# Gate and hid products by Strassen's scheme over 1024 tokens, with weights streamed per slice

## The chip, the cores and the metric

The kernel runs on one core of one Trainium2 chip. The metric is the device time of one launch in microseconds, as a median over runs. In the text PE is TensorE, ACT is ScalarE, DVE is VectorE, POOL is GpSimd, and SP is the queue that issues most DMAs.

## The reference

For 4 batches of 1024 tokens, 512 features each, the result is x plus one transformer block (all in float32):

```
x = x + attention(rmsnorm(x, t; g1, b1))          # 16 heads of 32
h = rmsnorm(x, t; g2, b2)                         # gain and bias from the condition t
y = (silu(h @ gate_w.T) * (h @ hid_w.T)) @ out_w.T    # hidden size 2048
out = x_in + (x + y)
```

The change touches only the second stage, from the second rmsnorm to the end.

## The kernel before

The kernel is two programs in sequence. `attention_program` computes the attention of all 4 batches and stores it to a DRAM tensor (`attn_out`). `ffn_program` does the rest. Each is a block in which every engine has its own instruction stream, with semaphores between them, written out by hand. Every product is taken with three matmuls: an operand is split into a rounded part (hi, written by ACT as float32r) and the rest (lo, written by DVE as full minus hi), and hi·hi, hi·lo and lo·hi are summed in PSUM.

`ffn_program` works on half batches of 512 tokens. At its start SP loads all weights: `wT` (gate and hid, 128 rows by 16 slices by 2 by 512) and `woT`. They stay in SBUF. Per half batch there are 16 slices `j` of 128 hidden units. In a slice:

- ACT rounds the two weight tiles of the next slice (L1113) and one of out_w (L1132); DVE takes the rests (L1189, L1211).
- PE makes two tiles of 128 by 512, gate and hid, with 4 k-tiles times 3 matmuls each, 24 in all (L1306), into a ring of four PSUM banks.
- ACT takes silu of gate from PSUM (L1137), DVE multiplies by hid from PSUM (L1217), ACT rounds the result (L1139), DVE takes its rest (L1221).
- PE adds the slice's part of the output product with 4 times 3 matmuls, 12 in all (L1287), one slice behind.

Beside this the next half batch is prepared: POOL adds x and attention, 128 by 2048 elements in one instruction, and the residual (L1084, L1086), ACT squares (L1102), DVE scales (L1170), and in slices 8 to 11 PE transposes one k-tile each (L1267, 16 transposes a half batch), which ACT and DVE split (L1107, L1180, L1183). After slice 15 DVE adds the four output banks to the residual (L1237) and SP stores them. For the first half batch this preparation stands ahead of the loop.

The first stage ends with 8 output tiles of 128 tokens (L776, L758), stored by SP; POOL issues the second stage's first loads while it ends (L420), each held back by a count of finished tiles, and waits for them at the end of its stream.

## Time and profile before

| | |
|---|---|
| median of 3 runs | 2622.42 us (2621.76 to 2624.55) |
| profiled execution | 2623.54 us |
| its span, first to last instruction | 2621.7 us |
| mean granted TensorE clock, share of full speed | 0.987 |
| second stage, first matmul of a slice to the last | 1547.6 to 2616.3 us |
| PE, DVE, ACT, POOL busy in that stretch | 1064.1, 544.7, 413.5, 88.2 us |

Durations of matmuls overlap: a matmul of 512 columns is shown as some 390 ns long, while one starts every 227 ns. What a stretch of them takes is to be read from start to start. "Idle before" is how long an engine stood still ahead of such an instruction, and what ended most of it.

### The profile page before, as it was taken

The numbers are of one execution on the slowest core, as the hardware profiler recorded it, in microseconds if no ns is written. First come the engines' busy times: TensorE is split into PE (matmuls) and PEld (weight loads), VectorE is DVE, ScalarE is ACT, GpSimd is POOL, SyncE is SP. The second block draws the span as 40 slices with busy tenths as digits, with TensorE's granted clock in tenths as the row PEclk, the third lists the DMA queues.
The fourth block names the chain that finished last, engine by engine and source line by source line (L and its number), as shares of the span: only waits on it lengthen the run. The fifth ranks groups of instructions, "written<-read, shape, count | busy, mean of one in ns | idle before, by whom it ended". The sixth has DMA issues, their size and how long they took to land. (4 is left out here: it accounts for less than half of the span.)

```text
span 2621.7 us, 38622 instructions
## 1 busy us (share of the span) xinstructions
PE 2474.9 (94%) x11764; PEld 1651.4 (63%) x11764; DVE 1478.8 (56%) x2316; ACT 1261.1 (48%) x2206; POOL 755.0 (29%) x557
## 2 busy tenths in 40 slices
PE   5999989999989999899999869999999999999999
PEld 4644437544446544365444448888888888888887
DVE  4766735667736667446677354554545454545454
ACT  4455662566653556625566524344434333343343
POOL 0255550455541555514555510000101010101010
PEclk8999999999999999999999979999999999999999
DMA  5222103212132112032121260101010101000000
GB/s 197 49 47 55 57 13 102 49 45 58 45 93 53 42 43 64 29 102 46 40 65 45 87 271 1 49 1 50 1 49 1 48 3 38 12 24 27 17 33 17
DMA packets 56685, 135.18 MB, mean 52 GB/s; under 512 B 11664, under 2 KB 11664, under 8 KB 53136
## 3 DMA queue, kind: packets, MB, share of 16 engines
q1 hardware_dynamic: 55920, 130.34, 16.7%
q8 instruction: 113, 1.85, 0.3%
q0 software_dynamic: 544, 2.10, 0.2%
q14 instruction: 108, 0.88, 0.1%
HBM read 59.78 MB, written 19.92 MB: 30 GB/s over the span
## 5 line engine op out<-in xcount | busy, mean ns | idle before, releaser
L409 POOL TENSOR_TENSOR sums<-probs 128x512 f32<-128x512 f32 x512 | 653.1, 1301 | 790.2 <-ACT probs L560 788.5
L633 DVE TENSOR_REDUCE pmax<-bank 128x1 f32<-128x512 f32 x1024 | 655.0, 685 | 279.5 <-PE bank L838 268.3
L560 ACT ACTIVATE probs<-bank 128x512 f32<-128x512 f32 x1024 | 584.1, 597 | 403.8 <-PE bank L921 370.2
L921 PE MATMUL bank<-qs,ks 128*128 128x512 f32 x1024 | 458.9, 453 | 29.2 <-ACT probs L560 28.5
L921 PEld LDWEIGHTS bank<-qs,ks 128*128 128x128 f32 x1024 | 191.3, 188 | 373.0 <-ACT probs L560 225.4
L838 PE MATMUL bank<-ks,qs 96*128 96x512 f32 x1024 | 401.1, 404 | 25.6 <-DVE pmax L633 25.5
L1306 PE MATMUL bank<-h_hi,gu_hi 128*128 128x512 f32 x1024 | 400.1, 391 | 9.3 <-DVE h_lo L1183 4.8
L1306 PE MATMUL bank<-h_hi,gu_lo 128*128 128x512 f32 x1024 | 399.5, 390 | 0.0
L1306 PE MATMUL bank<-h_lo,gu_hi 128*128 128x512 f32 x1024 | 399.4, 390 | 0.0
L1217 DVE TENSOR_TENSOR sg<-bank,sg 128x512 f32<-128x512 f32 x128 | 88.5, 691 | 385.2 <-PE bank L1306 385.2
L861 PE MATMUL bank<-probs,v 128*32 128x512 f32 x2048 | 275.9, 611 | 8.0 <-ACT o L492 5.3
L1139 ACT ACTIVATE a_hi<-sg 128x512 fp32r<-128x512 f32 x128 | 80.9, 632 | 386.9 <-DVE sg L1217 386.9
L838 PEld LDWEIGHTS bank<-ks,qs 96*128 96x128 f32 x1024 | 193.8, 189 | 73.0 <-DVE pmax L633 46.7
L1084 POOL TENSOR_TENSOR x<-x,res 128x2048 f32<-128x2048 f32 x8 | 38.2, 4770 | 668.5 <-DMA x<-attn_out 668.5
L1306 PEld LDWEIGHTS bank<-h_hi,gu_hi 128*128 128x128 f32 x1024 | 192.9, 188 | 51.5 <-issue 11.4
L1306 PEld LDWEIGHTS bank<-h_hi,gu_lo 128*128 128x128 f32 x1024 | 192.9, 188 | 40.2
L1306 PEld LDWEIGHTS bank<-h_lo,gu_hi 128*128 128x128 f32 x1024 | 192.9, 188 | 39.9
L1287 PE MATMUL bank<-wo_hi,a_hi 128*128 128x512 f32 x512 | 202.5, 396 | 0.0
L1287 PE MATMUL bank<-wo_hi,a_lo 128*128 128x512 f32 x512 | 199.6, 390 | 0.0
L1287 PE MATMUL bank<-wo_lo,a_hi 128*128 128x512 f32 x512 | 199.2, 389 | 0.0
L1189 DVE TENSOR_TENSOR gu_lo<-wT,gu_hi 128x512 fp32r<-128x512 f32 x258 | 188.2, 771 | 11.7 <-ACT gu_hi L1113 9.9
L1137 ACT ACTIVATE sg<-bank 128x512 f32<-128x512 f32 x128 | 76.3, 596 | 244.9 <-PE bank L1306 244.9
(108 smaller groups left out, 2767.4 us busy)
## 6 DMA issues: line engine op xcount, KB each, us to landing
ks<-qk_hi SPq DMA_DIRECT2D x136, 128.0 KB, 2.4
qs<-qk_hi SPq DMA_DIRECT2D x264, 64.0 KB, 2.0
x<-in_x SPq DMA_DIRECT2D x10, 1024.0 KB, 5.5
ks<-qk_lo SPq DMA_DIRECT2D x68, 128.0 KB, 2.4
qs<-qk_lo SPq DMA_DIRECT2D x132, 64.0 KB, 2.0
wv<-wv_parts SPq DMA_DIRECT2D x4, 2048.0 KB, 9.1
attn_out<-yout SPq DMA_DIRECT2D x32, 256.0 KB, 2.6
wT<-in_gu_w SPq DMA_DIRECT2D x8, 1024.0 KB, 14.2
```

The lines of the kernel that those rows point to most:

```text
L409: nc.gpsimd.tensor_tensor(sums[:, h, :], probs[:, 0, h, :], probs[:, 1, h, :], ALU.add) \
L560: nc.scalar.activation(probs[:, s % 2, h, :], sbank[i % SB][:], ACT.Exp, scale=SCALE).then_inc(st_done, 1)
L633: nc.vector.reduce_max(pmax[:, t, h, hf:hf + 1], mbank[n % MB][:], AX_X).then_inc(sq_done, 1)
L838: nc.tensor.matmul(mbank[n % MB][:], qs[0:96, u % 3, h, t * P:(t + 1) * P], ks[0:96, u // 2 % 2, h, hf * QB:(hf + 1) * QB], start=True, st ...
L861: last = nc.tensor.matmul(obank[DH * h:DH * h + DH, :], v[:, s, (g * GH + h) * DH:(g * GH + h + 1) * DH], probs[:, s % 2, h, :], start=(s ...
L921: nc.tensor.matmul(sbank[i % SB][:], ks[:, g % 2, h, s * P:(s + 1) * P], qs[:, u % 3, h, :], start=True, stop=True).then_inc(st_ready, 1)
L1137: nc.scalar.activation(sg[:, j % 2, :], psum[n % GU_BANKS][:], ACT.Silu).then_inc(g_act, 1)
L1139: nc.scalar.activation(a[0][:, j % 2, :], sg[:, j % 2, :], ACT.Copy).then_inc(ah, 1)
L1189: nc.vector.tensor_tensor(gu[1][:, slot, w, :, :], wT[:, j, w, :, :], gu[0][:, slot, w, :, :].bitcast(F32), ALU.subtract).then_inc(gul, 1)
L1217: nc.vector.tensor_tensor(sg[:, j % 2, :], psum[n % GU_BANKS][:], sg[:, j % 2, :], ALU.mult).then_inc(prod, 1)
L1287: last = nc.tensor.matmul(ybank[t][:], a[p][:, j % 2, t * P:(t + 1) * P], wo[q][:, j % 2, :], start=(j == 0 and p == 0 and q == 0), stop=( ...
L1306: last = nc.tensor.matmul(psum[n % GU_BANKS][:], gu[p][:, j % 2, w, k, :], hT[q][:, hf, k, :], start=(i == 0), stop=(i == len(steps) - 1))
```

## The change

The second stage now handles a whole batch of 1024 tokens at a time, in two phases.

Phase one, the gate and hid products. In each of the 16 slices the weights are a 2 by 2 matrix of blocks (gate or hid, by first or second half of the 512 features), and the activations are a 2 by 2 matrix (half of the features, by half of the tokens). Instead of 8 block products there are 7, each with 2 k-tiles times 3 matmuls, 42 in a slice for 1024 tokens. The operands are combinations. Those of the activations (`T1` to `T4`) are made once a batch by DVE; those of the weights (`S1` to `S4`) are made for every slice of every batch by POOL (`combos`), rounded by ACT in one instruction of 1024 columns, and their rests are taken by POOL too (`combos_lo`), eight POOL instructions of 128 by 256 a slice. The blocks used as they are (`A11`, `A12`, `A22`) are rounded by ACT and their rests taken by DVE (`weight_lo`). The seven products use four banks of one parity of `j`; three of the banks are used by two or three products in turn. ACT copies the first product out (`p1_copied`), and DVE makes seven sums with one operand in PSUM: `c11`, `u2`, `p5`, `c22`, `u3`, `c12`, `c21`. Then follow two silus on ACT (`gate1`, `gate2`) and two multiplications on DVE with both operands in SBUF (`gated`). Results for all 16 slices are kept in SBUF in full precision (`a`). The next batch's x and attention are added, squared and scaled in slices 4 to 7, 5 to 8 and 11 to 14, two tiles of 128 by 512 each; the adding is now DVE's.

Phase two, the output product, in 32 steps of 12 matmuls: 16 slices for the first 512 tokens, then 16 for the second. For each step ACT rounds a tile of `a` and one of out_w and DVE takes the rests, in rings of three. Beside it the next batch's 8 tiles are transposed, normalised by ACT (`full_tile`), combined by DVE and split. x and attention are loaded again for the residual.

Weights are no longer kept: SP loads 512 KB a slice (`load_raw`, a ring of three) and 256 KB an output step (`load_wo`, a ring of two). The lead prepares all 1024 tokens of batch 0, from four early loads in place of two. The core of the diff (both engines' loops in the middle of it without the removed lines, which are those printed above):

```diff
-                pool.wait_ge(sq_ready, NB * (NU * NMAX + NT) - NT + 3 * n + 1)
+                pool.wait_ge(sq_ready, NB * (NU * NMAX + NT) - NT + 2 * n + 1)
...
+A11, A12, A22, S1, S2, S3, S4 = range(NP)
+B11, B21, B22, T1, T2, T3, T4 = range(NP)
+PRODUCTS = ((A11, B11, 0), (A12, B21, 1), (S2, T2, 0), (S1, T1, 2), (S3, T3, 3), (S4, B22, 1), (A22, T4, 0))
+QUAD = ((0, 0), (2, 0), (2, 1), (0, 1))
+SPLIT_ORDER = (B11, B21, B22, T1, T3, T2, T4)
+T_ORDER = (T1, T3, T2, T4)
+TILES_AT = {q: (0, q) for q in range(4)} | {9 + q: (1, q) for q in range(4)}
+FULL_AT = {n + 2: tile for n, tile in TILES_AT.items()}
...
+                hold(sp, held, w_lo, b * (2 * NJ) + 2)
+                load_raw(2)
+                hold(sp, held, out_mm, b * STEPS + 1)
+                load_raw(3)
+                load_raw(4)
+                hold(sp, held, s_lo, b * (4 * NJ) + 8)
+                hold(sp, held, w_lo, b * (2 * NJ) + 4)
+                for s in y_stored:
+                    hold(sp, held, s, b * 32 + 16)
+                for hf in range(2):
+                    sp.dma_start(x1[:, TPH * hf:TPH * (hf + 1), :], tokens(attn, prepared, hf)).then_inc(x_loaded[hf], 16)
+                    sp.dma_start(xr[:, TPH * hf:TPH * (hf + 1), :], tokens(x, prepared, hf)).then_inc(x_loaded[hf], 16)
+                for j in range(5, NJ):
+                    hold(sp, held, w_lo, b * (2 * NJ) + 2 * (j - 2))
+                    hold(sp, held, s_step, b * (4 * NJ) + 4 * (j - 2))
+                    load_raw(j)
+                for n in range(STEPS):
+                    load_wo(b, n)
+                    if n == 2:
+                        load_raw(0)
+                    if n == 17:
+                        hold(sp, held, h_full, b * 8 + 16)
+                        for t in range(TPH):
+                            load_pair(b, 0, t)
+                    if n == 21:
+                        hold(sp, held, h_lo, b * (2 * NP) + 4 * NP)
+                        load_raw(1)
+                    if n >= STEPS - 6 and n < STEPS - 2:
+                        store(b, 0, n - (STEPS - 6))
+                    if n >= STEPS - 4:
+                        hold(sp, held, y_stored[n - (STEPS - 4)], b * 32 + 32)
+                        load_pair(b, 1, n - (STEPS - 4))
...
+            def combos(b, j, lead=False):
+                w = b * (4 * NJ) + 4 * j
+                src, to = raw_place(j), s_place(j, lead)
+                a11, a12, a21, a22 = src[:, 0, 0:2, :], src[:, 0, 2:4, :], src[:, 1, 0:2, :], src[:, 1, 2:4, :]
+                pool.wait_ge(raw_loaded[raw_sem(j)], raw_count(b, j))
+                nc.gpsimd.tensor_tensor(to[:, 0], a21, a22, ALU.add).then_inc(s_step, 1)
+                nc.gpsimd.tensor_tensor(to[:, 2], a11, a21, ALU.subtract).then_inc(s_step, 1)
+                pool.wait_ge(s_step, w + 1)
+                nc.gpsimd.tensor_tensor(to[:, 1], to[:, 0], a11, ALU.subtract).then_inc(s_step, 1)
+                pool.wait_ge(s_step, w + 3)
+                nc.gpsimd.tensor_tensor(to[:, 3], a12, to[:, 1], ALU.subtract).then_inc(s_step, 1)
...
+            def combos_lo(b, j, lead=False):
+                src, (hi, lo) = s_place(j, lead), wt[j % 2]
+                pool.wait_ge(w_hi, b * (3 * NJ) + 3 * (j + 1))
+                for i in range(4):
+                    nc.gpsimd.tensor_tensor(lo[:, S1 + i], src[:, i], hi[:, S1 + i].bitcast(F32),
+                                            ALU.subtract).then_inc(s_lo, 1)
...
+                for j in range(1, NJ):
+                    combos_lo(b, j)
+                    if j == 1:
+                        pool.wait_ge(out_mm, b * STEPS + 1)
+                    if j < NJ - 1:
+                        pool.wait_ge(s_lo, b * (4 * NJ) + 4 * (j + 1))
+                        combos(b, j + 1)
+                    if j == 11:
+                        inverse_root(b + 1)
+                pool.wait_ge(h_lo, b * (2 * NP) + 4 * NP)
+                combos(b + 1, 0)
+                combos_lo(b + 1, 0)
...
+            weight_hi(0, 0, True)
+            for t in range(8):
                 square(0, t)
+            for i in range(2):
+                for q in range(4):
+                    full_tile(0, i, q)
+                    if q < 3:
+                        h_rounded(0, i, (q,))
+                h_rounded(0, i, T_ORDER)
             with act.Fori(0, NB) as b:
+                for j in range(NJ):
+                    if j < NJ - 1:
+                        weight_hi(b, j + 1, False, (0, 1))
+                    act.wait_ge(prod_done, b * (NP * NJ) + NP * j + 1)
+                    nc.scalar.activation(a[:, j, 0, :], psum[4 * (j % 2)][:], ACT.Copy).then_inc(p1_copied, 1)
+                    if j < NJ - 1:
+                        weight_hi(b, j + 1, False, (2,))
+                    else:
+                        a_rounded(b, 0)
+                        wo_rounded(b, 0)
+                        wo_rounded(b, 1)
+                    act.wait_ge(c11_done, b * NJ + (j + 1))
+                    nc.scalar.activation(sg[:, j % 2, 0, :], sg[:, j % 2, 0, :], ACT.Silu).then_inc(gate1, 1)
+                    if 5 <= j < 9:
+                        square(b + 1, 2 * (j - 5))
+                        square(b + 1, 2 * (j - 5) + 1)
+                    act.wait_ge(c12_done, b * NJ + (j + 1))
+                    nc.scalar.activation(a[:, j, 1, :], a[:, j, 1, :], ACT.Silu).then_inc(gate2, 1)
...
+                for j in range(NJ):
+                    if j:
+                        c21(b, j - 1)
+                        gated(b, j - 1)
+                    u, e = a[:, j, 0, :], a[:, j, 1, :]
+                    bank = psum[4 * (j % 2):4 * (j % 2) + 4]
+                    if j < NJ - 1:
+                        weight_lo(b, j + 1)
+                    dve.wait_ge(prod_done, b * (NP * NJ) + NP * j + 2)
+                    dve.wait_ge(p1_copied, b * NJ + (j + 1))
+                    nc.vector.tensor_tensor(sg[:, j % 2, 0, :], bank[1][:], u, ALU.add).then_inc(c11_done, 1)
+                    dve.wait_ge(prod_done, b * (NP * NJ) + NP * j + 3)
+                    nc.vector.tensor_tensor(u, bank[0][:], u, ALU.add).then_inc(u2_done, 1)
+                    dve.wait_ge(prod_done, b * (NP * NJ) + NP * j + 4)
+                    dve.wait_ge(u2_done, b * NJ + (j + 1))
+                    nc.vector.tensor_tensor(e, bank[2][:], u, ALU.add).then_inc(p5_added, 1)
+                    dve.wait_ge(prod_done, b * (NP * NJ) + NP * j + 5)
+                    dve.wait_ge(p5_added, b * NJ + (j + 1))
+                    nc.vector.tensor_tensor(sg[:, j % 2, 1, :], bank[3][:], e, ALU.add).then_inc(c22_done, 1)
+                    nc.vector.tensor_tensor(u, bank[3][:], u, ALU.add).then_inc(u3_done, 1)
+                    if 4 <= j < 8:
+                        add_x(b + 1, 2 * (j - 4))
+                        add_x(b + 1, 2 * (j - 4) + 1)
+                    if j == 9:
+                        mean_square(b + 1)
+                    if 11 <= j < 15:
+                        scale_x(b + 1, 2 * (j - 11))
+                        scale_x(b + 1, 2 * (j - 11) + 1)
+                    if j == 13:
+                        set_norm(next_batch(b))
+                    if j == NJ - 1:
+                        a_rest(b, 0)
+                        wo_rest(b, 0)
+                        wo_rest(b, 1)
+                    dve.wait_ge(prod_done, b * (NP * NJ) + NP * j + 6)
+                    nc.vector.tensor_tensor(e, bank[1][:], e, ALU.add).then_inc(c12_done, 1)
...
+                pe.wait_ge(h_lo, b * (2 * NP) + 2 * NP)
+                for j in range(NJ):
+                    pe.wait_ge(w_lo, b * (2 * NJ) + 2 * (j + 1))
+                    pe.wait_ge(s_lo, b * (4 * NJ) + 4 * (j + 1))
+                    for n, (weight, h, place) in enumerate(PRODUCTS):
+                        bank = psum[4 * (j % 2) + place]
+                        if n == 0 and j < 2:
+                            pe.wait_ge(y_added, b * (2 * TPH) + TPH * (j + 1))
+                        elif n in (0, 1, 3, 4) and j >= 2:
+                            pe.wait_ge((c21_done, c12_done, p5_added, u3_done)[place], b * NJ + (j - 1))
+                        if n in (2, 5, 6):
+                            pe.wait_ge({2: p1_copied, 5: c11_done, 6: u2_done}[n], b * NJ + (j + 1))
+                        for i in range(2):
+                            for p, q in ((0, 0), (0, 1), (1, 0)):
+                                last = nc.tensor.matmul(bank[:], wt[j % 2][p][:, weight, i, :], H[q][:, h, i, :],
+                                                        start=(i == 0 and p == 0 and q == 0), stop=(i == 1 and p == 1))
+                        last.then_inc(prod_done, 1)
+                for n in range(STEPS):
+                    blk, j = n // NJ, n % NJ
+                    pe.wait_ge(a_lo, b * STEPS + n + 1)
+                    pe.wait_ge(wo_lo, b * STEPS + n + 1)
+                    if n == 0:
+                        for s in (c21_done, c12_done, p5_added, u3_done):
+                            pe.wait_ge(s, b * NJ + (NJ - 1))
+                    if n == NJ:
+                        pe.wait_ge(h_full, b * 8 + 16)
+                    for t in range(TPH):
+                        for p, q in ((0, 0), (0, 1), (1, 0)):
+                            last = nc.tensor.matmul(psum[4 * blk + t][:], aw[n % 3][:, p, t * P:(t + 1) * P], ow[n % 3][:, q, :],
+                                                    start=(j == 0 and p == 0 and q == 0), stop=(j == NJ - 1 and p == 1))
+                    last.then_inc(out_mm, 1)
+                    if n in TILES_AT:
+                        turn(b + 1, *TILES_AT[n])
```

Not shown: DVE's `combine` (one subtraction of 128 by 512 in SBUF for each of T1, T3, T2, T4, T2 after T1 and T4 after T2), `h_rest` (7 rests for each of two k-tiles), `add_x`, `scale_x`, `residual` and `finish` (one instruction a tile of 128 by 512), and ACT's `a_rounded` and `wo_rounded` (in step n they wait for output step n-3 to be done).

## Rows read from the trace of the kernel before

**Rows 1.** Page: busy time, share and instructions of each engine, whole span.

```profile
PE 2474.9 (94%) x11764; PEld 1651.4 (63%) x11764; DVE 1478.8 (56%) x2316; ACT 1261.1 (48%) x2206; POOL 755.0 (29%) x557
```

**Rows 2.** Chain that ended last, whole second stage, share by line.

```profile
by line: PE bank L1306 63.1%; PE bank L1287 31.2%; PE bank L1267 1.4%; issue 1.0%; DVE gu_lo L1189 0.6%; DMA wT<-in_gu_w 0.5%; DVE h_full L1180 0.3%; ACT junk L1102 0.3%; DVE res L1198 0.2%; DVE x L1170 0.2%; DVE res L1237 0.1%; DVEq L985 0
```

**Rows 3.** Windows: length; PE, PEld, DVE, ACT, POOL busy; clock, DMA share, GB/s.

```profile
1812.00:1946.00 134.00, 132.98 (x595) 109.77 (x594) 65.37 (x100) 53.52 (x94) 10.61 (x3) 1.00 0.07 25
1946.00:2078.50 132.50, 132.50 (x594) 109.68 (x593) 70.06 (x100) 50.84 (x92) 10.93 (x3) 1.00 0.07 25
```

**Rows 4.** Chain between 1806 and 1850 us: start, us, what.

```profile
1817.51 1.02 issue
1818.53 11.16 PE bank L1306 x48
1829.68 2.72 PE bank L1287 x12
1832.40 5.44 PE bank L1306 x24
```

**Rows 5.** Groups of instructions by line, second stage: busy, mean ns, idle before.

```profile
L1306 PE MATMUL bank<-h_hi,gu_hi 128*128 128x512 f32 x1024 | 400.1, 391 | 9.3 <-DVE h_lo L1183 4.8 <-issue 3.0 <-DVE gu_lo L1189 1.6
...
L1137 ACT ACTIVATE sg<-bank 128x512 f32<-128x512 f32 x128 | 76.3, 596 | 244.9 <-PE bank L1306 244.9
...
L1107 ACT ACTIVATE h_hi<-bank,bias_now,gain_now 128x512 fp32r<-128x512 f32 x36 | 27.5, 764 | 5.9 <-PE bank L1267 5.8
...
L1102 ACT ACTIVATE junk<-x 128x512 f32<-128x512 f32 x36 | 22.2, 617 | 0.3
```

**Rows 6.** ACT and POOL operations of other sizes.

```profile
L514 ACT ACTIVATE wq_hi<-wq_raw x1: 1910/1910/1910, 10.5 to 10.5; 128x2048 fp32r<-128x2048 f32 x1
...
L409 POOL TENSOR_TENSOR sums<-probs 128x512 f32<-128x512 f32 x512 | 653.1, 1301 | 790.2 <-ACT probs L560 788.5
...
L1084 POOL TENSOR_TENSOR x<-x,res 128x2048 f32<-128x2048 f32 x8 | 38.2, 4770 | 668.5 <-DMA x<-attn_out 668.5
```

**Rows 7.** DVE operations with one input in PSUM: duration min/median/max.

```profile
L625 DVE TENSOR_TENSOR qk_lo<-bank,qk_hi x67: 691/692/693, 34.0 to 1489.1; 128x512 fp32r<-128x512 f32 x67
...
L1217 DVE TENSOR_TENSOR sg<-bank,sg x128: 677/692/694, 1556.3 to 2611.0; 128x512 f32<-128x512 f32 x128
```

**Rows 8.** DVE operations with both inputs in SBUF: duration min/median/max.

```profile
L621 DVE TENSOR_TENSOR hT_lo<-hT_full,hT_hi x40: 684/693/1672, 17.9 to 1471.8; 128x512 fp32r<-128x512 f32 x40
...
L1221 DVE TENSOR_TENSOR a_lo<-sg,a_hi x128: 691/693/4625, 1557.7 to 2612.4; 128x512 fp32r<-128x512 f32 x128
```

**Rows 9.** POOL and DVE on the timeline near 1839 us: start, duration.

```profile
1838.90 4.62 POOL L1086 TENSOR_TENSOR res<-res,x 128x2048 f32<-128x2048 f32 x1
...
1839.45 4.62 DVE L1221 TENSOR_TENSOR a_lo<-sg,a_hi 128x512 fp32r<-128x512 f32 x1 [0.79 <-ACT a_hi L1139]
```

**Rows 10.** DVE on the timeline, 1562 to 1575 us.

```profile
1563.78 10.09 DVE L1189 TENSOR_TENSOR gu_lo<-wT,gu_hi 128x512 fp32r<-128x512 f32 x2
```

**Rows 11.** Lead of the second stage: chain of waits.

```profile
1525.06 5.31 DMA wT<-in_gu_w
...
1534.63 0.17 DVE var L1162
...
1539.16 1.13 PE bank L1267 x4
...
1547.62 13.96 PE bank L1306 x48
```

**Rows 12.** DVE timeline: last-but-one tile of the first stage, first additions of the second.

```profile
1518.87 0.69 DVE L758 COPY yout<-bank 128x512 f32<-128x512 f32 x1 [0.94 <-PE bank L776]
...
1525.35 2.49 DVE L1194 TENSOR_TENSOR x<-x,res 128x512 f32<-128x512 f32 x4
```

**Rows 13.** DMA issues: count, KB each, us to landing.

```profile
out<-res SPq DMA_DIRECT2D x32, 256.0 KB, 2.1
...
res<-in_x POOLq DMA_DIRECT2D x1, 1024.0 KB, 7.7
```

More of the change, by code:

```diff
@@ new lines, in ffn_program, with raw_place, raw_sem, raw_count @@
+    mhalf = at("mhalf2", [P, L // P], F32, "mhalf")
+    first, second = psum[0:4], psum[4:8]
+    def raw_place(j):
+        return raw_1 if j == 1 else raw_ring[0 if j == 0 else (j - 2) % 3]
+    def raw_sem(j):
+        return 3 if j == 1 else 0 if j == 0 else (j - 2) % 3
+    def raw_count(b, j):
+        users = [m for m in range(NJ) if raw_sem(m) == raw_sem(j)]
+        return b * (16 * len(users)) + 16 * (users.index(j) + 1)
+    def s_place(j, lead):
+        return s_lead if lead else s_01[j] if j < 2 else s_ring
@@ L1050, in _, with store @@
+            def store(b, blk, t):
+                hold(sp, held, y_added, b * (2 * TPH) + 2 * TPH + blk * TPH + t + 1)
+                rows = slice(blk * QB + t * P, blk * QB + (t + 1) * P)
+                sp.dma_start(out[b, rows, :], x1[:, t, :]).then_inc(y_stored[t], 16)
             for s in y_stored:
                 sp.sem_inc(s, 16)
-            sp.sem_inc(x_loaded, 16)
-            sp.sem_inc(attn_loaded, 16)
-            for kind, j in FFN_LOADS:
-                if kind == "gu":
-                    sp.dma_start(wT[:, j:j + GU_GROUP], gu_w[:, j:j + GU_GROUP]).then_inc(gu_loaded[j // GU_GROUP], 16)
-                else:
-                    sp.dma_start(woT[:, j:j + WO_GROUP, :], out_w[:, j:j + WO_GROUP, :]).then_inc(wo_arrived[j // WO_GROUP], 16)
+            load_raw(0)
@@ L1165, in scale_x @@
-            def scale_x(n):
-                dve.wait_ge(inv_ready, n + 1)
-                dve.wait_ge(summed, 2 * (n + 1))
-                for t in range(TPH):
-                    nc.vector.tensor_scalar(x1[:, t, :], x1[:, t, :], inv[:, t:t + 1], None, ALU.mult).then_inc(x_scaled, 1)
             def set_norm(nb):
@@ new lines, in mean_square, with scale_x, weight_lo @@
+            def mean_square(n):
+                dve.wait_ge(sq_sum, n * 8 + 8)
+                if not isinstance(n, int):
+                    dve.wait_ge(inv_ready, n)
+                nc.vector.tensor_scalar(var[:], ssq[:], 1.0 / D, EPS, ALU.mult, ALU.add).then_inc(var_ready, 1)
+            def scale_x(n, t):
+                dve.wait_ge(inv_ready, n + 1)
+                nc.vector.tensor_scalar(x1[:, t, :], x1[:, t, :], inv[:, t:t + 1], None, ALU.mult).then_inc(x_scaled, 1)
+            def weight_lo(b, j):
+                src, (hi, lo) = raw_place(j), wt[j % 2]
+                pieces = ((slice(A11, A12 + 1), src[:, 0].rearrange("p (a k) m -> p a k m", k=2)), (A22, src[:, 1, 2:4, :]))
+                for part, (to, full) in enumerate(pieces):
+                    dve.wait_ge(w_hi, b * (3 * NJ) + 3 * j + part + 1)
+                    nc.vector.tensor_tensor(lo[:, to], full, hi[:, to].bitcast(F32), ALU.subtract).then_inc(w_lo, 1)
@@ L1195, in _ @@
+            weight_lo(0, 0)
             mean_square(0)
[L1196 to L1205 removed]
@@ new lines, in _, with turn @@
+            pe.sem_inc(out_mm, 1)
+            def turn(n, i, q, lead=False):
+                if i == 1:
+                    pe.wait_ge(h_full, n * 8 + q + 1)
+                elif not lead:
+                    pe.wait_ge((c21_done, c12_done, p5_added, u3_done)[q], n * NJ)
+                if i == 0 and q == 0:
+                    pe.wait_ge(x_scaled, n * 8 + 8)
+                k, half = QUAD[q][0] + i, QUAD[q][1]
+                for t in range(TPH):
+                    last = nc.tensor.transpose(second[q][:, t * P:(t + 1) * P], x1[:, TPH * half + t, k * P:(k + 1) * P], ident[:])
+                last.then_inc(h_turned, 1)
```

517 lines of the change are left out of this document (258 added, 259 removed).

## The prediction

> **What bounds the kernel now.** I read the page first: PE is busy 94% of the span, DVE 56%, ACT 48%, POOL 29% [rows 1]. The chain of work that ended last then says where PE is the bound: over the whole second stage 63% of it is L1306 and 31% is L1287, both PE, and next to nothing is a wait [rows 2]. The windows of two half batches agree: PE is busy 132.98 of 134.0 and 132.5 of 132.5 us at a granted clock of 1.00, with DVE and ACT at about half [rows 3]. The chain between 1806 and 1850 us gives the unit: 24 matmuls take 5.44 us, 12 take 2.72, so one starts every 0.2267 us and a slice takes 8.16; at the turn from one batch to the next PE stands 1.02 us with nothing to wait for, and loses 0.28 more to a slower first slice [rows 4]. So a matmul less is worth 0.2267 us here, as long as DVE, ACT and POOL deliver in time.
>
> **What it removes.** Gate and hid for 1024 tokens took 2 x 16 x 24 = 768 matmuls a batch; seven products of six in 16 slices are 672. The output product stays at 384, the transposes at 32. 96 x 4 = 384 matmuls fewer, all of 512 columns: 384 x 0.2267 = **-87.1 us**. Also gone are POOL's instructions of 2048 columns. While two of them ran, two rests on DVE took 10.09 us [rows 10], and PE's next slice started late: after slice 2 (from 1564.3 to 1569.7) and output step 1 (to 1572.5), both counted on from the chain, DVE was only done at 1573.9. That is 1.4 us of standing and some 0.4 of slower matmuls: **-1.8 us**. It happened once.
>
> **The steady slice, by hand.** A slice now is 42 x 0.2267 = 9.52 us, a product 1.36. Count from its start, with 0.2 us from the last matmul of a product to the engine that waits. ACT's copy of product 1 runs 1.56 to 2.16 (0.60, as L1137 [rows 5]); product 3 overwrites that bank from 2.72, so there is 0.5 us to spare. ACT then rounds S1 to S4, 1024 columns: between 0.6 for 512 and 1.91 for 2048 [rows 5, 6], 1.05, until 3.2. POOL's operations have 256 columns, which no row shows. From 1.30 for 512 and 4.77 for 2048 [rows 6] the slope is 2.26 ns a column, so 0.72 us; above, it is bounded by the 1.30 of the 512. I take 0.72, since both rows are the same operation on the same types. Four rests run 3.25 to 6.1, four combinations for the slice after next 6.2 to about 9.1. PE wants the rests at 9.52. All in time.
>
> DVE: after product 7 the slice before's `c21`, two products of `gated` and two rests of weights, 0.6 us from start to start for 512 columns [rows 12], end at 3.0, when POOL stands still. `c11` and `u2` are due at 6.8 and 8.2 and done near 4 and 5. `c22` and `u3` start at 7.0, `c12` at 8.36. DVE is busy some 7 of 9.5 us, ACT 4.5. An operation with one input in PSUM does not care about POOL: L625 stays within 691 to 693 ns in 67 instances, with POOL at work beside it, and L1217 within 677 to 694 [rows 7]. So the seven sums cost nothing beyond their own time.
>
> The tight place is a chain over the slice's end: `c12` ends at 9.05, then on ACT silu 0.60, rounding of A11 and A12 0.62, of A22 0.40, and only behind these the copy of product 1, 0.60. It must end at 9.52 + 2.7 = 12.2. So `c12` may be 0.85 us late; what it is later, PE stands before product 3.
>
> **Slices 4 to 7** put two `add_x` ahead of `c12`, both inputs in SBUF. Such operations stand while POOL works: L1221 took 4.62 us beside a POOL instruction that ended at 1843.5, against 0.69, and L621 up to 1.67 [rows 8, 9]. The first one arrives at 8.2, when POOL has one or two of its eight left. In turns with POOL they end at 10.3, so `c12` starts 1.9 late and PE stands 1.0. In the next slice copy, rounding and POOL are shifted by this, so more of POOL lies under the adds: 1.3 each for three more. **5.0 us a batch, +20 in all.** Without a collision `c12` is 1.1 late, which costs 0.25 a slice, 4 in all. I take the first, as rows 8 and 9 show the block.
>
> **Slices 11 to 14** put two `scale_x` there, 0.4 us apart: `c12` is 0.7 late, which is covered. Whether this form, with one SBUF input, stands behind POOL is in no row: where the trace has this form (the scaling of x in both stages), POOL had ended or was just ending. If it did, by the reckoning above PE would stand 0.6 and three times 0.9, 3.3 a batch, 13 in all. I take 0. The Trainium skill (SBUF — State Buffer, section "Who interferes with whom") states that a tensor_scalar in its two-port mode takes the shared port pair for the whole instruction, and that one with two SBUF inputs contends with a POOL operation that reads SBUF; by this rule the sum is 13 us higher, which is a rival below. On the two inputs the trace agrees [rows 9].
>
> **Phase two.** A step is 2.72 us. ACT needs 1.2 (plus 1.4 beside a transposed tile), DVE 1.3 (plus at most 1.3): less than a step, and the rings of three leave two steps to spare. An out_w load has 256 KB; the store of that size lands in 2.1 us, the next larger, 1 MB, in 7.7 at the slow end [rows 13]. Taking 2.6: rests of step n-2, load, rounding, rests give 4.3 us for two steps of 5.44: hidden. At the start, step 1 waits for the late `c12` of slice 15, whose three extra rests cost 1.2 us: with the transposes between the steps it comes out even. I put **0.3 a batch, +1**. The batch turn keeps its 1.3 us: DVE's four last sums and two rests end before `c11` is due, and raw weights for slice 2, sent for after the stores, are wanted a slice later.
>
> **Lead.** Before, the stage's first DMA was issued at 1525.06 and slices began at 1547.62: 22.5 us [rows 11]. Now, from the stage's start: 512 KB land at 3.7 (between 2.1 and 5.31 [rows 11, 13]); POOL's combinations, in turns with DVE's eight adds, 8.1; ACT rounds them, 9.1; only then eight squares of 0.81 (0.617 and the read of the sum, [rows 5]), 15.6; mean, root and first scale 1.9, 17.5; eight scales 20.8; first tile on ACT 22.0. Then for each of two k-tiles ACT makes four full tiles and three roundings (0.76 and 0.6 [rows 5]) 5.1, DVE four combinations 2.6 and four rests 2.4, and the second k-tile reuses the first one's buffers: 10.1 twice. Start of slices at 42.1: **+19.6 us**. This is all on the path, since PE has nothing else. Bounds: 14, if the squares are not held back and the two k-tiles overlap in part, and 25, with raw weights late.
>
> The last of the four early loads waits for output tile 7 of 8, done at 1518.9 [rows 12]. With 7.7 us for such a load [rows 13] it lands at 1526.6, and the stage begins that late instead of at 1525.1: **+1.6 us** (0 to 3). The end is as before: four sums, four stores.
>
> **Sum.** -87.1 - 1.8 + 20 + 1 + 19.6 + 1.6 = -46.7 us. The profiled execution took 2623.5 us (span 2621.7 and 1.8 around it), 1.1 above the median of the runs, 2622.4. From the median: 2576 us.
>
> **Rivals.**
> - *No collision.* POOL ends before the adds arrive, as it would with operations of 0.6 us, or the order of arrival is kind. 4 in place of 20: 2560 us. For it: the overlap is only the last of eight operations. Against: 0.72 is worked out from rows at two sizes.
> - *The scales stand too*: 2589 us.
> - *POOL is the bound (slower).* Rounding S, four rests and four combinations are a loop from slice to slice: 1.05 + 0.3 + 8d. At d = 1.16 us it takes 10.65, 1.13 more than PE, and 60 slices eat the 68 us that stay of the gain without any other stall. At d = 1.30, the upper bound, it is 11.75: 60 x 2.2 = 134, so 2622 - 68 + 134 = 2688 us. For it: small POOL operations have a fixed share that no row isolates. Against: the two sizes show one of 0.14 us.
> - *Loads set the output steps.* If 256 KB took 4.8 us, two steps would take (4.8 + 1.7) in place of 5.44, +0.5 a step, 128 steps: +68, no gain, 2622 us. Against: DMA is at 7% in these windows [rows 3].
>
> **How the numbers follow.** Chances: forecast 0.36, no collision 0.22, scales too 0.22, POOL the bound 0.12, loads 0.08. The first three hold 0.8; the range reaches from the no-collision case with the lead at its lower bound (2553) to scales-too with the lead at its upper (2595), rounded out to 2550 to 2600. The likeliest alone is 2569 to 2583. About 0.2% (5 us) is what a measurement can tell from no change. Faster by more: the three, and the milder half of the two others, 0.87; within: 0.03; slower, mostly POOL: 0.10.
>
> **What would show it.** Steady slices (0 to 3, 9 to 11) 9.5 us apart on PE; a gap before the third product in slices 5 to 8, ended by ACT's copy; `add_x` over 0.69 us; POOL's operations of 256 columns at 0.72; some 42 us from the first raw load to the first slice; output steps 2.72 us apart. The forecast is wrong if POOL's operations are over 1.1 us, if all slices are stretched, or if output steps are paced by loads.

## The result and the profile after

The changed kernel takes 2608.02 us (median of 5 runs, 2601.17 to 2609.07) against 2624.55 us on the same chip (2621.76 to 2626.43): ratio 0.9926, 95% interval 0.9914 to 0.9938. It is faster, by 0.7%, where 2576 us were forecast and 2550 to 2600 as the range. The profiled execution has a span of 2606.2 us, 15.5 less than before, so some 31 us of the forecast gain are missing.

From the page of the changed kernel, busy time and share by engine, and the two new loads (count, KB each, us to landing):

```profile
span 2606.2 us, 39948 instructions
...
PE 2411.8 (93%) x11396; PEld 1584.0 (61%) x11396; DVE 1706.2 (65%) x2730; ACT 1321.3 (51%) x2289; POOL 1075.5 (41%) x1063
...
raw<-in_gu_w SPq DMA_DIRECT2D x66, 512.0 KB, 3.7
wo_raw<-in_out_w SPq DMA_DIRECT2D x128, 256.0 KB, 2.8
```

Against [rows 1] PE's busy time is 63 us less, and the share of its span 93%: it stands more. The matmuls themselves behave as forecast. The starts of ACT's copy of product 1, one a slice, in slices 3 to 5, 8 and 9 of the second batch (timeline of ACT; start, duration):

```profile
1876.42 0.60 ACT L1255 ACTIVATE a<-bank 128x512 f32<-128x512 f32 x1 [0.42 <-PE bank L1472]
...
1886.89 0.58 ACT L1255 ACTIVATE a<-bank 128x512 f32<-128x512 f32 x1
...
1897.31 0.58 ACT L1255 ACTIVATE a<-bank 128x512 f32<-128x512 f32 x1
...
1927.27 0.60 ACT L1255 ACTIVATE a<-bank 128x512 f32<-128x512 f32 x1 [0.42 <-PE bank L1472]
...
1936.79 0.60 ACT L1255 ACTIVATE a<-bank 128x512 f32<-128x512 f32 x1 [0.42 <-PE bank L1472]
```

1876.42 is the copy of slice 3, 1886.89 that of slice 4, and from there to slice 7 they are 10.42 apart; 1927.27 and 1936.79 (slices 8 and 9) are 9.52 apart. 42 x 0.2267 = 9.52: the saving of 87.1 us is there. What was lost stands in the changed kernel's view of waits (engine and line, what for, total us, times, longest), whole second stage:

```profile
ACT ow L1239 <- DMA wo_raw<-in_out_w: 79.8, 38, 5.8
...
DVE ow L1342 <- ACT ow L1239: 51.4, 32, 5.4
...
PEld bank L1472 <- ACT a L1255: 22.7, 29, 2.6
...
PE bank L1486 <- DVE ow L1342: 17.2, 10, 2.5
...
PE bank L1472 <- ACT a L1255: 11.1, 21, 2.1
```

The first line is new: 38 times ACT waited for a tile of out_w, 5.8 us at most, and DVE's rests and PE's steps behind it. The table below splits the profiled executions by phase, read from the starts of the copy of product 1 (slice 0 to 15, then slice 15 to the next batch's slice 0), for the changed kernel and the experiments that follow. The last column runs from the first load of weights in the second stage to the first copy. e7 is a single run.

| kernel | 15 slices, batches 0 to 3 | slice 15 to next slice 0 | lead |
|---|---|---|---|
| changed kernel | 148.2, 147.0, 147.0, 147.0 | 109.2, 107.8, 106.2 | 46.8 |
| e1 ring of four | 146.6, 147.0, 147.0, 147.0 | 101.2, 100.6, 100.8 | 46.7 |
| e2 spread | 146.6, 147.0, 147.0, 147.1 | 104.2, 105.1, 104.4 | 46.8 |
| e3 no pairs | 146.6, 147.0, 147.0, 147.0 | 101.8, 101.4, 101.4 | 46.8 |
| e5 small pairs | 146.6, 147.0, 147.0, 147.0 | 101.9, 102.3, 102.1 | 46.7 |
| e4 early loads | 148.2, 147.1, 147.1, 147.0 | 109.8, 110.2, 106.8 | 47.1 |
| e6 after c12 | 142.4, 142.8, 142.8, 142.8 | 107.1, 107.2, 108.7 | 46.7 |
| e7 half combinations | 142.6, 143.0, 143.0, 143.0 | 109.6, 107.9, 106.1 | 46.6 |
| e8 all parts | 142.4, 142.8, 142.8, 142.8 | 100.6, 100.7, 100.7 | 48.9 |

PE's own time for the third column is, by an estimate, 9.5 + 32 x 2.72 + 8 x 0.48 = 100.4: in the changed kernel's PE timeline a step with a transposed tile starts 3.18 to 3.21 us before the next one, 0.48 more than 2.72.

### The profile page after: what moved, and what is told of

It reads as the page before. It is cut to its first block and busy times, and to the rows that moved or that the text cites. A ratio compares the mean times of both kernels' runs of the same rounds, so it can differ in the third digit from the quotient of the medians.

```text
span 2606.2 us, 39948 instructions
## 1 busy us (share of the span) xinstructions
PE 2411.8 (93%) x11396; PEld 1584.0 (61%) x11396; DVE 1706.2 (65%) x2730; ACT 1321.3 (51%) x2289; POOL 1075.5 (41%) x1063
## 5 line engine op out<-in xcount | busy, mean ns | idle before, releaser
L921 PE MATMUL bank<-qs,ks 128*128 128x512 f32 x1024 | 458.9, 453 | 29.3 <-ACT probs L560 28.5
L838 PE MATMUL bank<-ks,qs 96*128 96x512 f32 x1024 | 402.6, 406 | 25.4 <-DVE pmax L633 25.3
L1486 PE MATMUL bank<-ow,aw 128*128 128x512 f32 x1536 | 367.6, 398 | 17.2 <-DVE ow L1342 17.2
L1472 PE MATMUL bank<-H_hi,wt_hi 128*128 128x512 f32 x896 | 353.8, 395 | 28.1 <-DVE H_lo L1332 14.6
L1472 PE MATMUL bank<-H_lo,wt_hi 128*128 128x512 f32 x896 | 350.0, 391 | 0.0
L1472 PE MATMUL bank<-H_hi,wt_lo 128*128 128x512 f32 x896 | 349.7, 390 | 0.0
L1486 PEld LDWEIGHTS bank<-ow,aw 128*128 128x128 f32 x1536 | 289.3, 191 | 82.3 <-issue 22.6
L1151 POOL TENSOR_TENSOR wt_lo<-s_ring,wt_hi 128x256 fp32r<-128x256 f32 x224 | 159.0, 745 | 200.8 <-ACT wt_hi L1198 200.8
L838 PEld LDWEIGHTS bank<-ks,qs 96*128 96x128 f32 x1024 | 193.9, 189 | 74.3 <-DVE pmax L633 46.8
L1472 PEld LDWEIGHTS bank<-H_hi,wt_hi 128*128 128x128 f32 x896 | 168.9, 188 | 75.1 <-ACT a L1255 22.7
L1472 PEld LDWEIGHTS bank<-H_hi,wt_lo 128*128 128x128 f32 x896 | 168.9, 188 | 35.8
L1472 PEld LDWEIGHTS bank<-H_lo,wt_hi 128*128 128x128 f32 x896 | 169.1, 189 | 34.2
L849 PE MATMUL bank<-sums,ones 128*32 128x512 f32 x1024 | 139.1, 616 | 0.9 <-POOL sums L409 0.9
```

The lines of the kernel that those rows point to most:

```text
L838: nc.tensor.matmul(mbank[n % MB][:], qs[0:96, u % 3, h, t * P:(t + 1) * P], ks[0:96, u // 2 % 2, h, hf * QB:(hf + 1) * QB], start=True, st ...
L849: last = nc.tensor.matmul(dbank[DH * h:DH * h + DH, :], ones[:], sums[:, h, :], start=(pair == 0), stop=(pair == PAIRS - 1))
L921: nc.tensor.matmul(sbank[i % SB][:], ks[:, g % 2, h, s * P:(s + 1) * P], qs[:, u % 3, h, :], start=True, stop=True).then_inc(st_ready, 1)
L1151: nc.gpsimd.tensor_tensor(lo[:, S1 + i], src[:, i], hi[:, S1 + i].bitcast(F32), ALU.subtract).then_inc(s_lo, 1)
L1472: last = nc.tensor.matmul(bank[:], wt[j % 2][p][:, weight, i, :], H[q][:, h, i, :], start=(i == 0 and p == 0 and q == 0), stop=(i == 1 and ...
L1486: last = nc.tensor.matmul(psum[4 * blk + t][:], aw[n % 3][:, p, t * P:(t + 1) * P], ow[n % 3][:, q, :], start=(j == 0 and p == 0 and q == ...
```

## Where the out_w loads are late

The changed kernel's timeline of SP's DMA queue around output step 17 of batch 0 (start, duration, line; x2 means two in a row):

```profile
1738.10 42.20 SPq L1069 DMA_DIRECT2D wo_raw<-in_out_w  x15
1780.63 0.35 SPq L1073 DMA_DIRECT2D x<-in_x  x1
1781.07 0.39 SPq L1074 DMA_DIRECT2D x<-attn_out  x1
...
1784.04 0.65 SPq L1074 DMA_DIRECT2D x<-attn_out  x1
1784.88 9.92 SPq L1069 DMA_DIRECT2D wo_raw<-in_out_w  x4
```

Between the out_w loads of steps 17 and 18 SP issues eight loads of 256 KB for the residual. The last of them is out at 1784.69 and the load of step 18 only then. ACT, which wants it, in the same kernel's timeline:

```profile
1784.83 0.63 ACT L1231 ACTIVATE aw<-a 128x512 fp32r<-128x512 f32 x1 [0.83 <-PE bank L1486]
1791.23 0.63 ACT L1239 ACTIVATE ow<-wo_raw 128x512 fp32r<-128x512 f32 x1 [5.77 <-DMA wo_raw<-in_out_w]
```

And the chain of work of that stretch:

```profile
1784.88 6.32 DMA wo_raw<-in_out_w
1791.23 0.64 ACT ow L1239
1791.89 0.70 DVE ow L1342
...
1792.73 15.46 PE bank L1486 x60
```

The load of step 18 took 6.32 us, where the median is 2.8: 2 MB lie ahead of it. So two lags add up, 4.3 us of issuing and 3.5 us of waiting in the DMA queues, and a ring of two, full 5.44 us ahead, doesn't cover them. The same happens in the last four steps, where each out_w load stands behind a store, a hold on that store and two loads. Added up over the four batches from PE's timeline, PE stood 8.6 us at step 18 and 10.7 us in the last steps and at the turn to the next batch.

Those 19.3 us are not the whole loss. In the chain above the 60 matmuls behind the stand took 15.46 us, where 60 x 0.2267 is 13.60. The windows of the changed kernel around that stand (columns as in [rows 3]) show why:

```profile
1793.20:1796.60 3.40, 3.40 (x9) 2.62 (x9) 3.06 (x5) 1.37 (x3) 1.43 (x2) 0.50 0.56 155
...
1796.60:1808.20 11.60, 11.60 (x52) 9.62 (x52) 8.03 (x11) 6.40 (x11) 5.86 (x7) 1.00 0.43 137
```

PE had stood 2.50 us, and just behind that its granted clock was 0.50, the lower of its two levels (1.2 in place of 2.4 GHz), and then full again. The same fall stands behind the second stand of batch 0 and behind both stands of batch 3, and behind none in batches 1 and 2, where PE stood up to 1.97 us at a time (the shorter ones of batches 0 and 3: 1.93 and 1.84). At 1.9 us each, the price of the first, the four falls cost some 7 us (an estimate): a stand of PE can cost almost twice its own length.

**Theory A** is that these loads hold up the out_w loads, and with them ACT, DVE and PE. **Theory B**: POOL's combinations for the next batch run in phase two as well, and DVE's rests stand behind them (1.2 us in place of 0.69 between 1804 and 1815). Four kernels tell them apart.

**e1_ring4**: every load two steps earlier, ring of four.

```diff
-    wo_raw = at("wo_raw2", [P, 2, QB], F32, "s_ring")
+    wo_pairs = [at("wo_raw2", [P, 2, QB], F32, "s_ring"), at("wo_raw3", [P, 2, QB], F32, "wo_b")]
...
-                    hold(sp, held, wo_lo, b * STEPS + n - 1)
+                elif n < 4:
+                    hold(sp, held, prod_done, b * (NP * NJ) + NP * NJ)
+                else:
+                    hold(sp, held, wo_lo, b * STEPS + n - 3)
...
+                load_wo(b, 0)
+                load_wo(b, 1)
                 for n in range(STEPS):
-                    load_wo(b, n)
+                    if n < STEPS - 2:
+                        load_wo(b, n + 2)
...
+    places["wo_b"] = places["wt_lo1"] + 8 * P
```

> Every out_w load is asked for two output steps earlier, into a ring of four in place of two; nothing else changes. Theory A (loads of out_w come late because SP has the residual's loads, which it issues in a row, ahead of them; in the changed kernel the second phase takes 97 to 100 us a batch where 91 is PE's own time, 28 us in all): the waits of ACT for out_w go and phase two takes 91 to 93 us; 20 to 27 us below the changed kernel, some 2580 us. Theory B (the rests on DVE stand behind POOL's combinations for the next batch, 1.2 us in place of 0.69 where both run in phase two): nothing of that is touched, within 3 us of the changed kernel's 2601 to 2609 us.

Measured: 2573.47 us, ratio to the kernel before 0.9802 (0.9782 to 0.9822). That is 34.5 us below the changed kernel, more than the 20 to 27 expected; of the 35.3 us between the two profiled spans, 5.0 are a second stage that began earlier and 1.6 a shorter slice 0, which this edit doesn't touch. The third column, which counts some 10 us more than the phase two of the expectation, falls from 107.7 to 100.9, PE's own time. The windows from slice 15's copy to the next batch's first copy (batches 0 and 1, columns as in [rows 3]) show it. Those of the changed kernel:

```profile
1729.15:1838.32 109.17, 104.59 (x459) 85.02 (x458) 74.61 (x114) 55.63 (x96) 12.87 (x12) 0.97 0.41 131
1985.35:2093.12 107.77, 101.66 (x459) 82.62 (x458) 76.62 (x115) 55.81 (x96) 12.67 (x12) 1.00 0.43 137
```

Those of this one:

```profile
1722.47:1823.71 101.24, 100.87 (x459) 82.92 (x458) 74.91 (x115) 55.35 (x96) 12.66 (x12) 1.00 0.44 142
1970.71:2071.27 100.56, 100.56 (x459) 82.92 (x458) 74.34 (x114) 55.23 (x96) 12.66 (x12) 1.00 0.45 142
```

The same 459 matmuls take 100.9 us of 101.2, with a clock of 1.00, although POOL does the same 12 operations in 12.66 us. They still collide with DVE: 4 of the 32 rests of out_w take up to 1.23 us in both batches here, as against 5 in the changed kernel. So what theory B blames is still there and costs nothing: it falls.

**e2_spread**: the eight loads of step 17 two by two.

```diff
                     if n == 17:
                         hold(sp, held, h_full, b * 8 + 16)
-                        for t in range(TPH):
-                            load_pair(b, 0, t)
+                    if 17 <= n < 17 + TPH:
+                        load_pair(b, 0, n - 17)
```

> Only the eight loads of x and attention that SP issues in a row after the out_w load of step 17 are spread, two behind each of steps 17 to 20. Theory A: the wait of 5 to 6 us for the out_w tile of step 18 goes, 4 to 5 us a batch, 16 to 20 us in all, some 2588 us; the waits at steps 28 to 31 stay. Theory B: no change.

Measured: 2589.83 us, ratio 0.9868 (0.9847 to 0.9888). In the third column 3.1 us a batch are won, 4 to 5 had been expected; 3.7 stay for the last steps.

**e3_no_pairs** raises the semaphore in place of the residual's loads, **e5_small_pairs** makes each of them 16 columns wide.

```diff
-                sp.dma_start(x1[:, t, :], x[b, rows, :]).then_inc(res_loaded[t], 16)
-                sp.dma_start(x1[:, TPH + t, :], attn[b, rows, :]).then_inc(res_loaded[t], 16)
+                sp.sem_inc(res_loaded[t], 32)                                                       # e3
+                sp.dma_start(x1[:, t, 0:16], x[b, rows, 0:16]).then_inc(res_loaded[t], 16)          # e5
+                sp.dma_start(x1[:, TPH + t, 0:16], attn[b, rows, 0:16]).then_inc(res_loaded[t], 16) # e5
```

> Leaves out the residual's loads of x and attention in phase two (16 DMAs of 256 KB a batch); their semaphore is raised without a load, so the output lacks the right residual. Theory A: all lateness of out_w goes, phase two takes 91 to 92 us, 25 to 28 us below the changed kernel, some 2578 us. Theory B: no change beyond 3 us.

> The residual's loads stay, as many and in the same places, but each moves 16 columns in place of 512 (the output lacks most of the residual). It tells apart what is late in theory A: if it is SP's own time to issue eight loads (4.3 us at step 17), most of the loss stays, some 2600 us; if it is the 2 MB that lie ahead of the out_w load in the DMA queues (that load took 6.3 us to land, against 2.8), about 3.5 us of each 6 go, some 2590 us or less.

Measured: e3 2574.15 us (0.9809, 0.9790 to 0.9828), e5 2579.92 us (0.9830, 0.9812 to 0.9847). Without the loads the third column is 101.5, with all 16 issues but hardly any data 102.1. So of the 6.2 us a batch that the loads cost (the falls of the clock behind the stands included), 5.6 go with their data; what SP needs to issue them costs 0.6. I take it that the ring covers the rest of the issuing; no run shows that by itself. My expectation for e5 had the split nearer to half.

## Why slices 4 to 7 and 11 to 14 are longer

The changed kernel's timeline of DVE in slices 4 and 5 of the second batch:

```profile
1883.06 1.82 DVE L1294 TENSOR_TENSOR x<-x,xr 128x512 f32<-128x512 f32 x2
1884.81 0.68 DVE L1417 TENSOR_TENSOR a<-bank,a 128x512 f32<-128x512 f32 x1
...
1893.16 2.15 DVE L1294 TENSOR_TENSOR x<-x,xr 128x512 f32<-128x512 f32 x2
```

POOL in the same stretch, its last operation of three slices:

```profile
1873.73 0.74 POOL L1141 TENSOR_TENSOR s_ring<-raw,s_ring 128x256 f32<-128x256 f32 x1
...
1883.27 1.07 POOL L1141 TENSOR_TENSOR s_ring<-raw,s_ring 128x256 f32<-128x256 f32 x1
...
1893.69 1.06 POOL L1141 TENSOR_TENSOR s_ring<-raw,s_ring 128x256 f32<-128x256 f32 x1
```

The additions arrive while POOL is at its last operations. Two of them take 1.82 us, then 2.15, where two without a collision take 1.29; and POOL's last operation grows from 0.74 to 1.07. The same in the groups by line (mean ns): POOL's fourth combination beside its third from 1550 us on, and additions and scalings from 1600 us on, without the eight of each in the lead, which take 684 and 482 ns.

```profile
L1141 POOL TENSOR_TENSOR s_ring<-raw,s_ring 128x256 f32<-128x256 f32 x56 | 48.1, 858 | 4.4
...
L1139 POOL TENSOR_TENSOR s_ring<-s_ring,raw 128x256 f32<-128x256 f32 x56 | 41.5, 742 | 0.0
...
L1294 DVE TENSOR_TENSOR x<-x,xr 128x512 f32<-128x512 f32 x32 | 33.1, 1075 | 0.0
...
L1304 DVE TENSOR_SCALAR x<-x,inv 128x512 f32<-128x512 f32 x32 | 22.0, 728 | 0.0
```

The scalings take 728 ns against some 480 before the change. They have only one input in SBUF, and take longer here all the same: that is what one of the rivals said.

**e6_after_c12** moves both behind `c12` (the same for `scale_x`).

```diff
-                    if 4 <= j < 8:
-                        add_x(b + 1, 2 * (j - 4))
...
                     dve.wait_ge(prod_done, b * (NP * NJ) + NP * j + 6)
                     nc.vector.tensor_tensor(e, bank[1][:], e, ALU.add).then_inc(c12_done, 1)
+                    if 4 <= j < 8:
+                        add_x(b + 1, 2 * (j - 4))
```

> The additions, mean, scalings and gain copies for the next batch stand behind c12 on DVE in place of ahead of it. Theory (PE stands before its third product because c12 is late, then silu, two roundings and the copy of product 1 behind it on ACT): slices 5 to 8 and 12 to 15 go back to 9.52 us, 147.0 us for 15 slices become 143 to 143.5, 14 to 16 us below the changed kernel, some 2590 us. Rival (DVE has too much to do in these slices, wherever it stands): the time stays within 3 us.

Measured: 2581.94 us, 0.9833 (0.9817 to 0.9849). 15 slices take 142.8, which is 15 x 9.52: nothing stands any more. That is 4.2 us a batch, 17 in all. The two profiled spans differ by 24.1: 16.8 of it are this, 1.6 a shorter slice 0 of the first batch, as in e1; 3.7 because the first load of weights came at 1530.41 in place of 1534.14, which has nothing to do with this edit either; of the other 2.0, 1.7 lie in the last batch's phase two. The collision itself is still there: the additions take 839 ns here (the scalings 479), but nobody waits for them.

**e7_half_combos** leaves out half the columns of POOL's four combinations in slices 3 to 15, so that POOL is done before the additions arrive; they stay ahead of `c12`.

```diff
+                c = 2 if isinstance(b, int) or j < 3 else 1
...
-                nc.gpsimd.tensor_tensor(to[:, 0], a21, a22, ALU.add).then_inc(s_step, 1)
+                nc.gpsimd.tensor_tensor(to[:, 0, 0:c], a21[:, 0:c], a22[:, 0:c], ALU.add).then_inc(s_step, 1)
...
```

> The four combinations that POOL makes for slices 3 to 15 in phase one take 128 of 256 columns (the other half of S1 to S4 is left as it was, so gate and hid products are not the reference's). POOL then ends near 7.9 us into a slice, before the additions arrive at 8.2. Theory (the additions stand behind POOL's operations): each pair takes 1.3 us in place of 1.8 to 2.2, the slices with additions take 9.6 to 9.9 us in place of 10.4, those with scalings 9.52 in place of 9.9 to 10.0; 15 slices take 143 to 144.5 us in place of 147.0. Rival (the additions cost their own time, POOL has no part in it): 147.0 stays.

Measured, one run: 2580.17 us, 15 slices in 143.0. The same additions and scalings, and POOL's half combination, in this kernel's groups by line:

```profile
L1142 POOL TENSOR_TENSOR s_ring<-raw,s_ring 128x128 f32<-128x128 f32 (+1 forms) x56 | 27.0, 482 | 4.4
...
L1295 DVE TENSOR_TENSOR x<-x,xr 128x512 f32<-128x512 f32 x32 | 21.1, 700 | 0.0
...
L1305 DVE TENSOR_SCALAR x<-x,inv 128x512 f32<-128x512 f32 x32 | 14.0, 478 | 0.0
```

700 and 478 ns: in the same place on DVE, with POOL out of the way, they cost 0.2 us a batch in place of 4.2. The collision with POOL is the cause, and `c12` is the place where it costs PE its time. The Trainium skill (SBUF — State Buffer, section "Who interferes with whom") has both forms contend with a POOL operation that reads SBUF, the tensor_scalar when it runs in a two-port mode. The traces agree that both stand, with 1075 against 700 ns for two SBUF inputs and 728 against 478 for the tensor_scalar; in which mode it ran, none of them shows.

## The end of the first stage and the lead

The first load of weights is issued at 1534.14 us, 9.1 later than in [rows 11]. Three of DVE's copies of the output tiles of the first stage, from the changed kernel's timeline:

```profile
1503.80 0.68 DVE L758 COPY yout<-bank 128x512 f32<-128x512 f32 x1
...
1516.06 0.69 DVE L758 COPY yout<-bank 128x512 f32<-128x512 f32 x1 [9.06 <-DMA attn_out<-yout]
...
1528.79 0.69 DVE L758 COPY yout<-bank 128x512 f32<-128x512 f32 x1 [1.94 <-PE bank L776]
```

The third copy waited 9.06 us for the store of an earlier tile, where its counterpart before waited 6.09, and from the last copy's start to the first weights there are 5.35 us where there were 3.55 (1521.51 to 1525.06). The first copy itself, in code that is unchanged, was at 1503.80 here and at 1499.70 before; over the other profiles it lies between 1497.3 and 1503.0, so 4.1 of the 9.1 us tell nothing of the change.

**e4_early** issues two early loads as before, at the counts of before, and lets SP load the rest in the second stage.

```diff
-                pool.wait_ge(sq_ready, NB * (NU * NMAX + NT) - NT + 2 * n + 1)
+                pool.wait_ge(sq_ready, NB * (NU * NMAX + NT) - NT + 3 * n + 1)
...
-             for hf in range(2) for to, src in ((x1, attn), (xr, x))]
+             for hf in range(1) for to, src in ((x1, attn), (xr, x))]
...
             load_raw(0)
+            sp.dma_start(x1[:, TPH:, :], tokens(attn, 0, 1)).then_inc(late_loaded, 16)
+            sp.dma_start(xr[:, TPH:, :], tokens(x, 0, 1)).then_inc(late_loaded, 16)
```

> The first stage again issues only two early loads, at the counts of finished tiles of the kernel before (1 and 4); the second half of x and attention of batch 0 is loaded by SP in the second stage, behind the first raw weights. Theory: the early loads hold back the stores of the last output tiles and the end of the first stage (in the changed kernel 30.3 us lie between the DVE copy of output tile 0 and the first raw load, in the kernel before 25.4). Expected 25.4 to 26, the lead itself (first raw load to first slice, 40.9 us) at most 1 us longer: 4 to 5 us below the changed kernel, some 2601 us. Rival: the first stage's end only varies from run to run: no change.

Measured: 2603.58 us, 0.9904 (0.9884 to 0.9924). From the first copy to the first weights: 24.9 us, against 30.3 and, before, 25.4; the wait of the third copy is 6.80 us. Over all kernels this stretch is 28.4 to 30.3 us with four early loads and 24.9 to 26.6 with two. The place is as the theory has it, but the edit changes two things, the number of early loads and when the second one goes out (1.8 us behind the first copy in the changed kernel, 4.7 in e4 and before), and no run separates them. By the medians alone (intervals 0.9914 to 0.9938 and 0.9884 to 0.9924 overlap) the gain is not certain.

**e8_best** joins e1, e4 and e6, and in the lead puts ACT's eight squares ahead of its rounding of S.

```diff
-            weight_hi(0, 0, True)
+            weight_hi(0, 0, True, (0, 1))
             for t in range(8):
                 square(0, t)
+            weight_hi(0, 0, True, (2,))
```

> All together: ring of four for out_w asked for two steps earlier, two early loads, additions and scalings behind c12, and in the lead the eight squares ahead of the rounding of S1 to S4. Gains of the single parts: 27 (ring), 4 to 5 (early loads), 15 (behind c12), and 4 for the squares, which no longer wait for POOL's combinations. Expected 2556 to 2560 us; if the gains overlap, up to 2566.

Measured: 2557.61 us, 0.9745 (0.9731 to 0.9760). The time is inside what was expected, but partly by luck: the lead grew to 48.9 us instead of falling, and what the slices and the ring gave above their 15 and 27 us (18.4 and 28.5 in the profiles of e6 and e1) made up for most of it. On POOL the root of the mean stands behind the four rests of S, and these now waited for ACT (POOL's timeline):

```profile
1542.87 2.77 POOL L1162 TENSOR_TENSOR wt_lo<-s_lead,wt_hi 128x256 fp32r<-128x256 f32 x4 [6.70 <-ACT wt_hi L1209]
1545.60 1.66 POOL L1156 TENSOR_TENSOR inv<-var,mhalf 128x8 f32<-128x8 f32 x1
```

**e9_best2** puts the root ahead of the four rests; **e10_no_squares** is e8 without the move of the squares.

> The version with all parts, and in the lead POOL takes the root of the mean before the four rests of S1 to S4, in place of after them. With the squares ahead of the rounding of S, the root stood 3.5 us behind these rests, and the lead (first raw load to the copy of product 1) took 48.9 us, more than the 46.8 and 47.1 without the reordering. Expected 45.4 us for the lead, 3.5 us below the version with all parts: 2554 us. If the end of the lead is set by the splitting of the tiles alone, no change, 2557 us.

> The version with all parts, but the squares again behind the rounding of S1 to S4. If the reordering of the squares cost 1.8 us by pushing the root back, the lead is 47.1 us and the time 2556 us; if the 48.9 us came from elsewhere (the loads of the second half of x), it stays.

Measured: e9 2553.89 us (0.9734, 0.9715 to 0.9754), lead 47.6; e10 2555.18 us (0.9735, 0.9711 to 0.9758), lead 47.1. e10 did what was expected. The time of e9 is the 2554 expected, but not by its mechanism: its lead did not reach 45.4, and the two chains of the lead show why. That of e9:

```profile
1529.02 9.00 DMA xr<-in_x
...
1541.64 1.67 POOL inv L1156
...
1543.34 5.13 DVE x L1318 x8
```

That of e10:

```profile
1529.83 9.24 DMA xr<-in_x
...
1543.80 1.67 POOL inv L1156
...
1545.49 3.27 DVE x L1317 x8
```

Counted from the first load of weights (1528.14 and 1528.95 us), the root came 1.4 us earlier in e9, but POOL's rests then ran beside the eight scalings, and those took 5.13 us in place of 3.27: 0.5 us more in all, as in the two leads. And in both the second half of x lands only at 1538 to 1539, 9 us after it was asked for, with the other loads around it. e8, e9 and e10 are not told apart by their intervals; any of them beats both kernels, by 2.5 to 2.7% the one before.

## Why the prediction was wrong, step by step

- **The saving, -87.1**: right. A slice without extras takes 9.52 us.
- **Slices 4 to 7, +20, and 11 to 14, 0**: the mechanism was right, and by luck the sum too. Both together cost 4.2 us a batch, 17 in all: the additions 3.3 a batch, 13 against 20 (a slice with them takes 10.4 to 10.5 us, and the one behind them only 9.1, which gives 0.4 back), and the scalings 1.0 a batch, 4 against 0, since they collide too. The rival that had them do so put 13 us on them.
- **POOL's operations at 0.72**: 0.74 measured, so the rival in which POOL is the bound has no ground.
- **The lead, +19.6**: from the first load to the first slice 40.9 us (1534.14 to 1575.00), forecast 42.1; but ACT then waited for the second slice's weights and PE stood 2.1 us in the first slice, which I had not seen. That slice took 15.1 us in place of 9.5, since PE also came out of the lead at the lower clock (0.66 from 1574 to 1580 us, 0.91 from 1580 to 1600); the kernel before paid for that too, with 13.96 us for 48 matmuls in place of 10.88 [rows 11].
- **The first stage's end, +1.6**: 9.1 in this profile. The last load costs 1.8, as forecast; about 3 more (30.3 - 25.4 - 1.8) go with the early loads, four of them and the second one sooner, beside which the first stores land later (11.3 us after their issue, 8.3 before), a step that I left out; the remaining 4.1 were there before the first copy and are not the change's.
- **Phase two, +1**: this is the step that failed, the overlap of the out_w loads with two output steps. By the difference to e1 it cost 8.0, 7.2 and 5.4 us in the first three batches; the last batch, whose matmuls end at 2600.55, has 8.0 more than e1's by the same count: 28.6 us, against 1; some 19 of it are PE standing and some 7 the lower clock behind four of the stands, a price for which the forecast had no term. I wrote that two steps of 5.44 us cover 4.3 of load and rounding, with a landing of 2.6 (2.8 measured). That sum holds for a load with nothing ahead of it. I did not walk SP's queue through phase two, where 16 DMAs of 256 KB a batch stand between the out_w loads. My rival on loads had the right place, but asked whether a lone 256 KB load takes 4.8 us everywhere, and the mean use of the DMA engines (7%) was no evidence against a queue of 2 MB at one spot.

The sum with what was measured: -87.1 (matmuls) - 1.8 (as forecast, not measured by itself) + 16.8 (slices 4 to 7 and 11 to 14) + 28.6 (phase two) + 18.4 (lead: 19.6 less the 1.2 it was shorter) + 2.1 (first slice) + 9.1 (start of the stage) = -13.9, and the span fell by 15.5. One term is missing: I kept the turn of the batches, and PE, which stood 1.02, 1.14 and 0.84 us at the three turns before, stands 0.37, 0 and 0 us in e1. With it the sum is -16.5; 1.0 us stays open.

## What to carry to other kernels

A stream that used to be resident and now comes through a small ring is only as safe as the worst moment of the queue that carries it: walk that queue instruction by instruction, and count the bytes ahead of each load, not only the load's own landing time. Asking for it earlier (a ring of four in memory that was free) made the stretch as short as leaving the other loads out (100.9 us, and 101.5 in e3), with no less traffic. A stand of PE is not paid off when it ends: look at the granted clock just behind it. And before an instruction is put on the path that frees a bank, look at what POOL is doing at that moment: behind `c12` the same work collided still, and cost PE nothing.

## What the runs showed of the hardware that was not expected

- A 256 KB load behind 2 MB of others on the same queue landed after 6.3 us; the median of the 128 such loads is 2.8.
- A DVE tensor_scalar with one SBUF input stands behind a POOL operation: eight took 5.13 us with POOL at work and 3.27 without.
- Stores of 256 KB issued by SP land late beside large loads. The first store of an output tile, with a 2 MB load of SP's ahead of it, landed after 11.3 us in the changed kernel and 10.8 in e6, and after 9.0 in e4 and e8, where POOL's second 1 MB load went out later and the third not at all; the last stores of e4, with no load beside them, took 2.0.
- After a stand of 2.50 us PE's granted clock was 0.50 for a while, and 60 matmuls took 15.46 us in place of 13.60. It fell behind four of the stands in the changed kernel, and stands of 1.8 to 2.0 us in batches 1 and 2 passed without it.
